# Mixture-of-experts kernel: VectorE makes both parts of two input groups, and two other groups are transposed ahead of the second routing step

## The chip, the core and the metric

The kernel runs on one core of a Trainium2 chip as one program. The metric is the device time of one execution in microseconds (us), lower is better. Engines are named as the profile names them: PE is TensorE (matmuls and transposes, its weight loads are PEld), DVE is VectorE, ACT is ScalarE, POOL is GpSimd and SP is SyncE, which here only issues DMAs.

## What is computed

The reference is a chain of two layers, each a conditioning stage and a feed-forward stage. The part that matters here is the second layer's conditioning, a mixture of experts with a shared branch:

```python
shared_out = silu(x_flat @ sw1.T) * (x_flat @ sw3.T) @ sw2.T
s = sigmoid(x_flat @ router_w.T + t_bias)            # 4096 tokens, 8 experts
topk_idx = top_k(s + router_bias, 2)
gates = s[topk_idx] / sum(s[topk_idx])
H = gelu(x_flat @ rw1[e].T); O = H @ rw2[e].T        # for the two experts of a token
out = (shared_out + sum_of_chosen(gates * O)) / 3
```

`x` is 16 sequences of 256 tokens of width 256. Before it come a recurrence of 256 steps with a router and a top-2 mixture of wide experts; after it a quantised feed-forward layer.

## The kernel before

The 4096 tokens are 32 tiles of 128 tokens, or 8 groups of 4 tiles. The recurrence takes up about the first 400 us, the first mixture's expert tiles run to 760 us, the second mixture from 760 to about 1000, and the quantised layer to the end. Each engine runs its own instruction stream in the order in which the program writes it; semaphores are the only ties between the engines. In the second mixture that order is written out by hand, in `mixture_pe`, `mixture_act`, `mixture_dve` and `mixture_pool`.

What happens to a group g before the expert tiles:

- SP loads `x1`, the layer's input, in 16 halves of groups (two per group, 256 KB each, L2071), at most four in flight.
- The input is split in two f16 parts. `input_hi` (L996, ACT) writes the high part of each half group and counts `xn_hi`; `input_lo` (L1208, DVE) waits for it, writes the low part and counts `xn_lo`. When eight low parts are done SP also loads the held expert weights, 2 MB, over the part of `x1` that was read (L2084).
- `transposes` (L846, PE) turns both parts, through two PSUM banks, and `input_T` (L1007, ACT) copies each back, counted by `xs_T`. A bank is free for the next group once its copy is made.
- `router` (L833, PE) multiplies the transposed group by the router's weights.

Routing goes in three steps over groups 0 to 1, 2 to 3 and 4 to 7. A step is 30 DVE operations (`mix_route_op`, L1128 to L1191): operation 0 reads the router's sums; ACT's `sigmoid` (L1053) comes between operations 0 and 1; after operation 14 PE's `mix_ranks` (L864, L868) counts the tokens of each expert, which operation 26 (L1178) reads; operation 29 (L1191) writes `mslot_of`, the destinations of the step's tokens. Then POOL scatters the rows of its groups to the experts' places in memory, 8 indirect DMAs a group, 64 in all (L1634), in the order of the groups.

The shared branch is cut in units: units 0 to 7 are the four pairs of hidden parts of group 0 (even units times `sw1`, odd ones times `sw3`). PE computes a unit into one of four banks. For an even unit ACT applies Silu (L1024, with a table load ahead of the first), for an odd unit DVE multiplies (L1229, waits for the Silu and for PE), then ACT makes the high part of the result (`hi_part`, L1014, issued behind the next even unit's Silu) and DVE the low part (`lo_part`, L1214). Units 8 and 9 belong to group 1, units 10 to 13 are outputs of group 0.

From unit 40 on PE takes up the expert tiles, 39 slots of tokens of one expert, with the remaining units between them. SP loads a tile's rows (L2115, or L2110 and L2112) once the scatters of groups 0 to 5 have landed (48 of the 64); PE transposes (L936) or takes a DMA transpose, computes both products (L833), DVE weighs the output with the gates (L1319) into one of three buffers, and POOL scatters it by up to two indirect DMAs (L1642, 71 in all). A buffer is free when its scatter has landed. When all 71 have landed SP loads the results back (L2132), DVE combines them, and the quantised layer follows.

## Time and profile before

| | |
|---|---|
| time, median of 3 runs | 1107.3 us (1105.65 to 1110.83) |
| time of the profiled execution | 1105.51 us, its span 1103.7 |
| busy PE, weight loads | 951.4 us (86%), 749.5 (68%) |
| busy DVE, ACT, POOL | 774.1 (70%), 542.8 (49%), 374.3 (34%) |
| mean granted clock of TensorE | 0.821 of full speed |
| input loads of the second mixture | from 765 us |
| its first expert tile | 856 us |
| results loaded back | from 972 us |

The busy shares are averages over stages with different limits. The chain of work that ended last is followed back from the last instruction, at each step to what released it. A row of a timeline gives start, length, engine, line, operation, tensors and count, and in brackets the idle time just before and what ended it. The granted clock is a share of 2.4 GHz, 0.50 is 1.2 GHz.

### The profile page before, as it was taken

Reading aid. Unit: us, or ns where it says so; the run is one execution under the profiler, and the core shown is the slowest. Engines: PE = TensorE matmul, PEld = TensorE weight load, DVE = VectorE, ACT = ScalarE, POOL = GpSimd, SP = SyncE. Lnnn points to the kernel's source line nnn. Section 1 sums busy time; section 2 is a strip of 40 time slices with the busy share of each in tenths; the row PEclk is TensorE's granted clock in tenths of the full one; section 3 lists DMA queues with packets and bytes.
Section 4 is the critical chain, followed back from the end, with each engine's and each line's share of the span. In section 5 each row is a group of like instructions: output and inputs, shape, how many; then the busy total and the mean of one; then the engine's idle time right before and its main releaser. Section 6 shows DMA issues by size and latency. Waiting matters only on the chain.

```text
span 1103.7 us, 29587 instructions
## 1 busy us (share of the span) xinstructions
PE 951.4 (86%) x9662; PEld 749.5 (68%) x9663; DVE 774.1 (70%) x2791; ACT 542.8 (49%) x1764; POOL 374.3 (34%) x412
## 2 busy tenths in 40 slices
PE   6777777777777699999999999997789999896787
PEld 5566665666656588888888888886455666573354
DVE  5676767767677676889656566654673697778977
ACT  4555555555555533333334334434643666536496
POOL 1001121211212356743433233332477667721000
PEclk7555555555555699999999999998899999998999
DMA  8322332323323345954843453544635779583024
GB/s 247 93 83 77 100 94 79 116 78 101 94 78 116 107 86 105 209 103 92 148 69 57 63 67 58 67 69 96 211 108 182 181 180 204 153 287 114 1 39 115
DMA packets 136266, 124.91 MB, mean 113 GB/s; under 512 B 80161, under 2 KB 115746, under 8 KB 135938
## 3 DMA queue, kind: packets, MB, share of 16 engines
q1 hardware_dynamic: 115010, 83.36, 29.6%
q0 software_dynamic: 21120, 39.77, 16.0%
q8 instruction: 80, 1.31, 0.5%
q14 instruction: 56, 0.46, 0.1%
HBM read 62.88 MB, written 56.87 MB: 109 GB/s over the span
## 4 chain that ended last, share of the span: by engine, by line
PE 55%; DVE 18%; ACT 10%; issue 7%; POOL 5%; DMA 4%; SPq 0%; DVEq 0%; POOLq 0%
PE ps L1706 15%; PE ps L1716 15%; PE ps L2349 8%; DVE ps L2276 6%; PE ps L2354 5%; PE ps L833 4%; ACT work L2200 4%; ACT ps L2195 4%; POOL mrows L1634 3%; DVE imax L1542 3%; PE ps L1438 2%; PE ps L2319 2%; POOL mresults L1642 2%; PE ps L2327 1%; DVE lane L1814 1%
## 5 line engine op out<-in xcount | busy, mean ns | idle before, releaser
L1735 ACT ACTIVATE lane<-ps,b_now 128x256 f32<-128x256 f32 (+1 forms) x312 | 141.0, 455 | 239.2 <-PE ps L1706 223.1
L1706 PE MATMUL ps<-lane,W 128*128 128x256 f16 (+1 forms) x1872 | 197.6, 264 | 1.5 <-issue 0.9
L1716 PE MATMUL ps<-W,lane 128*128 x1704 | 192.9, 273 | 0.8 <-DVE lane L1814 0.5
L1706 PEld LDWEIGHTS ps<-lane,W 128*128 x1872 | 170.9, 98 | 24.2 <-issue 4.1
L1716 PEld LDWEIGHTS ps<-W,lane 128*128 128x128 f16 x1704 | 165.3, 98 | 22.2 <-issue 1.7
L1896 POOL DMA_INDIRECT results<-lane,dest x71 | 113.8, 1603 | 194.5 <-DVE lane L1800 136.6
L2349 PE MATMUL ps<-work 128*128 128x16 f16 x2048 | 98.9, 177 | 86.7 <-ACT work L2200 86.1
L2349 PEld LDWEIGHTS ps<-work 128*128 128x128 f16 x2048 | 76.2, 107 | 138.3 <-ACT work L2200 136.9
L1814 DVE TENSOR_TENSOR lane<-lane 128x256 f16<-128x256 f32 (+1 forms) x312 | 125.7, 403 | 10.8
L1866 POOL DMA_INDIRECT rows<-work,slot_of x64 | 63.5, 992 | 156.4 <-DVE ps L2276 152.4
L1812 DVE CAST lane<-lane 128x256 f16<-128x256 f32 (+1 forms) x312 | 92.5, 297 | 20.3 <-ACT lane L1735 20.0
L2292 DVE TENSOR_TENSOR work<-ps,work 128x32 f16<-128x32 f32 x256 | 49.0, 191 | 78.3 <-ACT ps L2202 78.1
L2319 PE MATMUL ps<-work 128*128 128x128 f32 x256 | 97.7, 487 | 5.8 <-DVE work L2240 4.9
L2276 DVE TENSOR_TENSOR_SCAN ps<-ps,work 128x64 f32<-128x64 f32 x256 | 76.4, 299 | 30.6 <-ACT ps L2195 7.9
L833 PE MATMUL ps<-W,work 128*128 128x512 f16 x384 | 91.4, 385 | 3.3 <-issue 2.5
L2259 DVE SCALAR_TENSOR_TENSOR work<-ps,alpha,work 128x16 f32<-128x16 f32 x510 | 93.4, 225 | 0.0
L2195 ACT ACTIVATE ps<-ps 128x32 f32<-128x32 f32 x256 | 46.6, 182 | 93.9 <-PE ps L2354 93.9
L2200 ACT ACTIVATE work<-ps 128x32 f16<-128x32 f32 x256 | 50.6, 198 | 75.2 <-DVE ps L2276 73.9
L1800 DVE SCALAR_TENSOR_TENSOR lane<-ps,b_now 128x512 f32<-128x512 f32 (+1 forms) x39 | 25.1, 643 | 88.5 <-PE ps L1716 88.5
L1642 POOL DMA_INDIRECT mresults<-lane,mdest x71 | 72.5, 1021 | 28.1 <-issue 15.6
L2190 ACT ACTIVATE W<-stage 128x128 f16<-128x128 f32 x256 | 78.7, 307 | 0.0
L2300 DVE SCALAR_TENSOR_TENSOR W<-stage,W 128x128 f16<-128x128 f32 x256 | 71.7, 280 | 0.0
(299 smaller groups left out, 1548.8 us busy)
## 6 DMA issues: line engine op xcount, KB each, us to landing
stage<-in_w1T SPq DMA_DIRECT2D x16, 512.0 KB, 3.8
stage<-in_w2T SPq DMA_DIRECT2D x16, 512.0 KB, 4.2
b_now<-in_b SPq DMA_DIRECT2D x39, 128.0 KB, 2.9
W<-mrows SPq DMA_DIRECT2D x16, 260.0 KB
work<-in_zT SPq DMA_DIRECT2D x32, 128.0 KB, 2.2
results<-in_xn SPq DMA_DIRECT2D x32, 128.0 KB
W<-results SPq DMA_DIRECT2D x16, 256.0 KB, 4.1
W<-mresults SPq DMA_DIRECT2D x4, 1024.0 KB, 9.2
```

What stands on the lines that cost most here:

```text
L833: last = pe.matmul(dst, lhs(a, k), rhs(b, k), start=(n == 0 and k == ks[0]), stop=(n == 2 and k == ks[-1]))
L1642: pool.indirect_dma_start(out=mresults_d, in_=mout[:, b, q], in_offset=None, out_offset=bass.IndirectOffsetOnAxis(ap=mdest[:, n % GATE_BUF ...
L1706: last = pe.matmul(ps[:, f % 4, 0:wide], of_e(W1[:, bass.ds(e, 1), a, k, f * P:(f + 1) * P]), xrows[:, b, k], start=(i == 0 and k == 0), s ...
L1716: last = pe.matmul(ps[:, 4 + q, 0:D], hid[:, a, f, q * P:(q + 1) * P], of_e(W2[:, bass.ds(e, 1), b, f]), start=(i == 0 and f == 0), stop=( ...
L1735: act.activation(v4[:, f % 4, 0:wide], ps[:, f % 4, 0:wide], ACT.Relu, bias=b1_now[:, p, f:f + 1], scale=A_SCALE / W_SCALE).then_inc(l1_v, 1)
L1814: dve.tensor_tensor(lo, v, hi, ALU.subtract).then_inc(l1_hid, 1)
L1896: pool.indirect_dma_start(out=results_d, in_=obuf[:, p, q], in_offset=None, compute_op=ALU.add, out_offset=bass.IndirectOffsetOnAxis(ap=de ...
L2200: act.activation(hring[:, j % 2, 0, :, c:c + BATCH], u[:, :, :, 1], ACT.Tanh, scale=0.5)\
L2259: dve.scalar_tensor_tensor(zs[:, j % 2, c // BATCH, k, :, 1], h[:, k], alpha[:, k:k + 1], z[:, j, k, c:c + BATCH], ALU.mult, ALU.add).then ...
L2276: dve.tensor_tensor_scan(ps[:, 5, 0:2 * DB], ps[:, 6, 0:2 * DB], zs[:, j % 2, s % STEPS_PER_TILE].rearrange("p c b v -> p (c b v)"), 0.0, ...
L2319: pe.matmul(dst, wz[:, k, cols], z[:, slot, k, :], start=(k == 0), stop=False, skip_group_check=True)
L2349: pe.matmul(ps[:, b + m, c:c + BATCH], w[:, k, m * P:(m + 1) * P], hring[:, prev, 0, k, pc:pc + BATCH], start=False, stop=False, skip_grou ...
```

## The change

Six edits, all in the order of the second mixture before its expert tiles.

1. The high parts of groups 2 and 3 (halves 4 to 7) are made by DVE in `input_lo`, by a tensor_scalar ahead of each low part, and counted by a semaphore of their own, `xn_hi_v`. ACT no longer makes them. `hi_set` gives the semaphore and the count for a half.
2. DVE takes the inputs of groups 0 to 3 ahead of step 0 of the routing; before, groups 2 and 3 came behind it.
3. DVE stops after operation 14 of step 0 for units 0 and 1; before, they came behind the whole step and the low parts of groups 2 and 3.
4. DVE takes the low parts of groups 4 and 5 ahead of step 1; before, those of 4 to 7 came behind it. Those of 6 and 7 come behind it now.
5. PE transposes groups 2 and 3 ahead of unit 0, and groups 4 and 5 ahead of `mix_ranks(1)`; the units and `mix_ranks(0)` stand around them as the diff shows.
6. ACT copies the transposes of groups 2 and 3 and makes the high parts of groups 4 and 5 ahead of unit 0; it copies groups 4 and 5 ahead of `sigmoid(1)`, and makes the high parts of 6 and 7 behind it, ahead of unit 4.

```diff
+        def hi_set(i):
+
+            if i < 4:
+                return xn_hi, i + 1
+            return (xn_hi_v, i - 3) if i < 8 else (xn_hi, i - 3)
...
-                        pe.wait_ge(xn_lo if s else xn_hi, 2 * g + h + 1)
+                        pe.wait_ge(*((xn_lo, 2 * g + h + 1) if s else hi_set(2 * g + h)))
...
             for g in (0, 1):
                 router(g)
-            units(0, 3)
-            mix_ranks(0)
-            units(3, 4)
             for g in (2, 3):
                 transposes(g)
-            units(4, 5)
+            units(0, 2)
+            mix_ranks(0)
             for g in (2, 3):
                 router(g)
-            units(5, 7)
-            mix_ranks(1)
-            units(7, 8)
+            units(2, 4)
             for g in (4, 5):
                 transposes(g)
-            units(8, 9)
+            units(4, 7)
+            mix_ranks(1)
+            units(7, 9)
             for g in (6, 7):
                 transposes(g)
             units(9, 10)
...
             sigmoid(0)
             for g in (2, 3):
-                input_hi(g)
-            units(0, 2)
-            for g in (2, 3):
                 input_T(g)
-            units(2, 4)
-            sigmoid(1)
             for g in (4, 5):
                 input_hi(g)
-            units(4, 6)
+            units(0, 4)
+            for g in (4, 5):
+                input_T(g)
+            sigmoid(1)
             for g in (6, 7):
                 input_hi(g)
-            for g in (4, 5):
-                input_T(g)
-            units(6, 8)
+            units(4, 8)
             for g in (6, 7):
                 input_T(g)
...
-                    dve.wait_ge(xn_hi, i + 1)
+                    if 4 <= i < 8:
+                        dve.wait_ge(x_in[i % 4], 16 * (i // 4) + 16)
+                        dve.tensor_scalar(rows_[:, :, 0:D], x1[:, 2 * i:2 * i + 2], A_SCALE, None, ALU.mult).then_inc(xn_hi_v, 1)
+                    dve.wait_ge(*hi_set(i))
...
-            for g in (0, 1):
+            for g in (0, 1, 2, 3):
                 input_lo(g)
-            ops(0, 0, MIX_OPS)
-            for g in (2, 3):
+            ops(0, 0, 15)
+            units(0, 2)
+            ops(0, 15, MIX_OPS)
+            for g in (4, 5):
                 input_lo(g)
-            units(0, 2)
             ops_and_units(1, 2, 3, 4, 5)
-            for g in (4, 5, 6, 7):
+            for g in (6, 7):
                 input_lo(g)
```

## Rows read from the trace of the kernel before

**Rows 1.** Chain of work that ended last, 740 us to the end, by line.

```profile
by line: PE ps L833 13.3%; issue 11.4%; POOL mrows L1634 10.6%; DVE imax L1542 7.8%; PE ps L1438 5.6%; POOL mresults L1642 5.2%; DMA mresults<-lane,mdest 3.0%; DMA stage<-mresults 2.8%; PE ps L1426 2.5%; PE ps L1716 2.2%; DMA results<-lane,
```

**Rows 2.** POOL's timeline, 757 to 1000 us (start, length, operation, idle before).

```profile
784.57 1.19 POOL L1634 DMA_INDIRECT mrows<-W,mslot_of  x1 [21.73 <-DVE mslot_of L1191]
...
801.27 1.50 POOL L1634 DMA_INDIRECT mrows<-W,mslot_of  x1 [0.30 <-issue]
...
848.18 1.01 POOL L1634 DMA_INDIRECT mrows<-work,mslot_of  x1 [0.30 <-issue]
...
884.88 0.97 POOL L1642 DMA_INDIRECT mresults<-lane,mdest  x1 [3.07 <-DVE lane L1319]
```

**Rows 3.** POOL by line, 784 to 870, 870 to 896, 896 to 971 us: busy, idle before.

```profile
L1634 POOL DMA_INDIRECT mrows<-W,mslot_of x32 | 34.0, 1062 | 31.2 <-DVE mslot_of L1191 21.7 <-issue 8.8 <-DVE W L1154 0.6
L1634 POOL DMA_INDIRECT mrows<-work,mslot_of x32 | 32.1, 1004 | 9.8 <-issue 9.8
...
L1642 POOL DMA_INDIRECT mresults<-lane,mdest x16 | 16.0, 999 | 10.2 <-DVE lane L1319 6.9 <-issue 3.4
...
L1642 POOL DMA_INDIRECT mresults<-lane,mdest x56 | 57.5, 1026 | 18.2 <-issue 12.5 <-DVE lane L1319 3.8 <-DVE mdest L1300 1.8
```

**Rows 4.** SP's timeline, and L2071's issue to landing.

```profile
774.21 4.96 SPq L2071 DMA_DIRECT2D W<-results  x6
...
786.84 0.36 SPq L2084 DMA_DIRECT2D W<-rweights  x1
...
852.00 0.39 SPq L2115 DMA_DIRECT2D W<-mrows  x1
...
DMA to landing us min/median/max: 2.8/4.1/4.5
```

**Rows 5.** PE's timeline, 757 to 880 us.

```profile
800.26 1.97 PE L846 MATMUL ps<-identh,work 128*128 128x128 f16 x16 [3.07 <-DVE work L1208]
...
809.24 2.56 PE L833 MATMUL ps<-rw_s,W 128*128 128x8 f16 x96
...
856.31 0.61 PE L936 MATMUL ps<-identh,W 128*128 128x128 f16 x8
```

**Rows 6.** ACT's timeline, 757 to 880 us.

```profile
773.45 1.94 ACT L1007 ACTIVATE W<-ps 128x1024 f16<-128x1024 f16 x2 [0.21 <-PE ps L846]
...
776.71 2.17 ACT L996 ACTIVATE W<-W 128x512 f16<-128x512 f32 x4
778.90 1.28 ACT L1024 ACT_TABLE_LOAD   x1
780.19 0.60 ACT L1024 ACTIVATE lane<-ps 128x512 f32<-128x512 f32 x1
...
790.46 0.26 ACT L1053 ACTIVATE W<-W 128x64 f32<-128x64 f32 x1 [0.62 <-DVE W L1128]
```

**Rows 7.** DVE's timeline, 757 to 880 us.

```profile
770.78 1.36 DVE L1208 SCALAR_TENSOR_TENSOR W<-W 128x512 f16<-128x512 f32 x2 [0.84 <-ACT W L996]
776.29 0.23 DVE L1128 SCALAR_TENSOR_TENSOR W<-ps,t_bias 128x64 f32<-128x64 f32 x1 [4.15 <-PE ps L833]
...
780.48 0.29 DVE L1154 TENSOR_TENSOR W<-W 128x128 f32<-128x128 f32 x1
...
784.12 0.17 DVE L1191 CAST mslot_of<-W 128x16 uint32<-128x16 f32 x1
...
799.43 4.90 DVE L1208 SCALAR_TENSOR_TENSOR work<-W,work 128x512 f16<-128x512 f32 x8
...
811.84 0.29 DVE L1128 SCALAR_TENSOR_TENSOR W<-ps,t_bias 128x128 f32<-128x128 f32 x1 [0.24 <-PE ps L833]
```

**Rows 8.** DVE by line and shape, whole span: count, busy, mean ns.

```profile
L2241 DVE TENSOR_SCALAR work<-work 128x512 f16<-128x512 f32 x1 | 0.4, 419 | 0.0
```

**Rows 9.** Stretches: length, busy PE, PEld, DVE, ACT, POOL; clock, DMA share, GB/s.

```profile
776.00:779.00 3.00, 3.00 (x17) 1.12 (x15) 2.04 (x10) 2.44 (x6) 0.00 (x0) 0.50 0.92 260
...
776.00:812.00 36.00, 27.42 (x332) 17.20 (x330) 26.18 (x84) 24.27 (x36) 21.64 (x20) 0.90 0.51 171
```

More of the change, by code:

```diff
@@ L462, in build_program @@
         xn_hi = sem("xn_hi")
+        xn_hi_v = sem("xn_hi_v")
         xn_lo = sem("xn_lo")
```

## The prediction

> **What bounds the kernel now.** I read the chain of work that ended last from 740 us on, then each engine's timeline over 757 to 880 us, then GpSimd's (POOL's) own queue to the end of the mixture. The chain view shows that POOL's scatter instructions of L1634 are, with 10.6%, the second largest named part of the last 364 us and that those of L1642 add 5.2% [rows 1]. POOL's timeline says why: it issues nothing until the destinations of step 0 are there (21.73 us idle, first scatter at 784.57), and from then on one every 1.28 us [rows 2]. The grouped rows count 64 of L1634 and 71 of L1642 and little idle time other than the 0.30 us between issues; only between 870 and 896 does POOL wait for VectorE (DVE), 6.9 us, and 3.8 us after that [rows 3]. So two serial things run side by side: POOL's 135 scatters, which start when step 0 of the router is done, and TensorE (PE), which reaches the tiles at 856.31 without idle time [rows 5]. They meet twice. SyncE (SP) may load the rows of tile 0 only when 48 scatters have landed; the 48th is issued at 848.18 and SP's load at 852.00 [rows 2, 4]. And at the end 71 results must be out. PE is the pacemaker of the tiles until about 896, where POOL waits for it; before the tiles it has slack only as far as tile 0's rows allow, at most 856.31 - 852.00 = 4.3 us for their landing.
>
> **The change part by part.** All times are those of the profiled run (span 1103.7, time 1105.51, 1.8 below the median of 1107.3); the difference found is added to the median.
>
> *VectorE's new operations.* Four tensor_scalar of 128x512 f32 to f16. The same form takes 419 ns at L2241 [rows 8]; about 0.04 us of waiting for its own semaphore follows, and the low part goes on at 4.90 / 8 = 0.61 us each [rows 7]. So 4 x (0.46 + 0.61) = 4.3 us, begun when the low parts of groups 0 and 1 are done, about 772.1 (770.78 + 1.36) [rows 7]. The data is there: SP's load 10 (counted from 0), issued at 774.21, waited for load 6, so the last of the four halves lands about 774.9 and none is later than DVE's turn by more than 0.1 us [rows 4]. DVE ends at 776.4; today it waits 4.15 us for the router until 776.29 [rows 7]. Cost 0.1 us, cover complete. If the operation ran at the pace of the low part (0.69 us) it would cost 1.2 us; below nothing is excluded, since step 0 can't begin before the router's sums.
>
> *ScalarE (ACT) is relieved of* the four high parts of groups 2 and 3 (2.17 us at 776.71) [rows 6], but what follows matters more. Today it goes on to the table load (1.28) and the first Silu, done at 780.79 [rows 6]. Now it does sigmoid(0) until 776.8 (today its next operation starts at 776.71), then four copies of transposes, then the four high parts of groups 4 and 5, and only then units 0 and 1. PE makes the first half of group 2's transposes from 776.1 at the low clock (granted 0.50, so 1.2 GHz) [rows 9], 8 in 1.05 us; copies follow at 777.2, 778.3, 779.4 and 780.4, PE and ACT taking turns as they do for group 1 (two copies in 1.94 us) [rows 6], and end at 781.4. High parts until 783.5, table load until 784.8, Silu until 785.4.
>
> *Destinations of step 0.* DVE now stops after 15 operations of step 0 for units 0 and 1. Unit 1 needs that Silu: 785.4 instead of no wait at all, for DVE reached this place at 780.48. It takes 0.61 us, and the other 15 operations take 784.29 - 780.48 = 3.8 us [rows 7]. Destinations at 789.8, first scatter at 790.1 instead of 784.57: **+5.5 us** on POOL. PE is not what ends this wait: its units 0 and 1 are done at 783 at the high clock, at 785.5 if the clock stayed low, so the term holds either way within 0.5 us.
>
> The rows give the table load 1.28 us with the Silu right behind it [rows 6]. The Trainium skill (ScalarE: Activation LUTs, What ACT_TABLE_LOAD costs) adds a drain of about 1.38 us to each switch. This trace doesn't show that part; by the page the term would be 6.9 us.
>
> *Step 1 and 2 behind it.* Low parts of groups 4 and 5 (2.45 us) end at 792.3; PE waits for the first of them inside transposes(4), from 787.9 to 790.5. ACT's last copy of group 5 ends at 794.4, sigmoid(1) starts there instead of 790.46 [rows 6]. From sigmoid(1) to the end of step 1 is 9.0 us today (790.46 to 799.43) [rows 6, 7]; unchanged, since the extra unit waits are met: destinations at 803.4. POOL needs them 16 scatters after 790.1, at 811. Then low parts of 6 and 7 (2.45), unit 5 and its high part (1.2), four copies (4.1), router of groups 4 to 7 (2.56) [rows 5] and hand-overs: the first operation of step 2 at about 814.0 instead of 811.84 [rows 7], destinations some 11 us later (30 operations, an estimate from their spacing of 0.26 to 0.35 us in this timeline), at 825; POOL needs them 32 scatters after 790.1, at 833 [rows 3]. Both are covered, by 8 us each.
>
> *TensorE.* Of 36 us from 776 to 812 it is busy 27.42 [rows 9], 8.6 idle. In the new order I find idle 2.6 (transposes(4)), 1.1 (group 5), 1.8 (mix_ranks(1) at 798.9), 1.9 (transposes(6)) and 3.4 us (transposes(7), whose copy stands behind unit 6's high part on ACT), 10.8 in all: **+2.2 us** at the tiles, 858.5. After 3.07 us idle today, 16 transposes took 1.97 us [rows 5]; one or two such slow stretches may add 1 us each. They are covered by the next term.
>
> *Tile 0's rows.* The 48th scatter moves by 5.5 less what POOL's pace gains. Two scatters of 1.50 us lie beside the eight low parts of 799.43 (the one of 801.27 stands for both) [rows 2, 7]; today 12 low parts run beside POOL's scatters, then 8. I take 0.5 us off, bounds 0 and 1.1 (both long ones gone). The Trainium skill (SBUF — State Buffer, Who interferes with whom) says that such an operation with two SBUF inputs contends only with a GpSimd instruction that reads SBUF, and a tensor_scalar in its two-port mode with any; by it the new operations harm nothing, as POOL is idle then, and the gain would be nothing or all of it. SP's load of tile 0 goes to 857.0. Its landing isn't in the trace: at most 4.3 us as above; the 256 KB loads of x took 2.8 to 4.5 [rows 4]. I take 3.5, as scatters run beside it: rows at 860.5, PE at 856.3 + **4.2** (2.9 to 5.5).
>
> *SP.* The 2 MB load at 786.84 [rows 4] waits for eight low parts, now done at 776.4, and goes out behind the last x load, about 782.7. It ends before most scatters: nothing on the path.
>
> *End.* From the tiles to 896 PE paces and POOL waits for it, so the last scatter moves with PE, and the loads, the combination and the last stage follow serially. Sum +4.2: 1107.3 + 4.2 = **1111.5**.
>
> **Rivals.** (a) *POOL's own pace decides* (slower): the tiles' rows and every mout buffer hang on POOL, so the whole +5.5 arrives, or 6.9 with a longer way to the Silu: 1112.8 to 1114.5. For it: 56 scatters after 896 go almost without a wait [rows 3]. Against it: 10.7 us of waits for DVE since 870. It decides if the shift of the first scatter is over 5.5.
> (b) *The delay is absorbed* (not slower): if POOL waits less between 870 and 896 as it comes later (up to 6.9 us there) and tile 0's rows take 2.8 us, only PE's own shift is left; if PE's gaps also come out smaller than mine, that shift is 0 to 2.2: 1107.3 to 1109.5. For it: the slack is in the rows. Against it: tile 0 hangs on scatter 48, ahead of the slack.
> (c) *Faster*: sooner transposes fill PE's gaps and the Silu isn't late, so destinations come at 784.3 as now. Of the 8.6 us idle the 3.07 before transposes(4) [rows 5] would go: 1104.2. It needs ACT to reach unit 0 by 779.2, and its queue forbids that.
> (d) *Nothing of the order matters*, within 1 us of 1107.3: would need step 0's second half to be off every chain; the 21.73 us wait for it speaks against it.
>
> **Chances.** Forecast (+2.5 to +5.5) 0.55; (a) 0.23; (b) with (d) 0.16; (c) 0.06. About 0.5%, 5.5 us, is what a measurement of this kernel can tell from no change. Over that slower: all of (a) above 1112.8, and a little of the forecast's edge, 0.27; faster by it: only a (c) larger than found, 0.04; within: 0.69. The range leaves out (c) and the upper end of (a) by noise: 1107.0 to 1114.5.
>
> **What would show it.** First scatter near 790.1 and a DVE wait of about 4.8 us for ScalarE ahead of unit 1; high parts by DVE of about 0.42 us between 772 and 776.4; SP's load of tile 0 near 857; an idle time of about 2 us of PE ahead of the first tile transposes; the last scatter near 974. The prediction is wrong if unit 1 is read before 782, if the load of tile 0 goes out before 854, or if PE reaches the tiles later than its rows.

## The result, and the profile after

| | before | after |
|---|---|---|
| time, median of 20 runs each | 1106.95 us (1104.99 to 1110.83) | 1109.88 us (1107.22 to 1111.28) |
| ratio after to before | | 1.0020, 95% interval 1.0011 to 1.0028 |
| time of the profiled execution, its span | 1105.51, 1103.7 | 1109.46, 1107.5 |

By the ratio the change costs 2.2 us (1.2 to 3.1). The two medians are 2.9 us apart; here and below a cost in us is worked out from the ratio, which has the interval. The forecast was +4.2, 1111.5, on a base of 1107.3: the direction was right, the size was about twice what came and lies outside the interval. The prediction took some 5.5 us as the least that a measurement of this kernel can tell from no change; with 20 runs each the interval is about 1 us to either side. Of all executions below one, of pe_late, fell in a slow state (1181.64 us); it stands in that run's median and in no ratio.

One thing for every comparison below: the stages before the second mixture don't end at the same time in two executions. I take the start of DVE's copy that opens the second mixture as a mark and subtract its offset. In the profile after the offset is 0.64 us. "Net" means with the offset taken off; the rows are raw.

POOL's timeline of after: start, length, operation, idle before. The first scatter comes at 790.17 net instead of 784.57 [rows 2], 5.6 us later.

```profile
790.81 1.19 POOL L1639 DMA_INDIRECT mrows<-W,mslot_of  x1 [27.12 <-DVE mslot_of L1192]
792.30 1.50 POOL L1639 DMA_INDIRECT mrows<-W,mslot_of  x1 [0.30 <-issue]
...
852.53 0.96 POOL L1639 DMA_INDIRECT mrows<-work,mslot_of  x1 [0.30 <-issue]
...
972.11 0.97 POOL L1647 DMA_INDIRECT mresults<-lane,mdest  x1 [0.31 <-issue]
```

DVE's timeline of after. The four high parts take 0.42 us each (one row stands for them), operation 0 starts behind them without a wait, and unit 1 waits 4.85 us for the Silu. The change has moved DVE's wait from ahead of step 0 (4.15 us, [rows 7]) to the middle of it.

```profile
773.94 0.42 DVE L1210 TENSOR_SCALAR W<-W 128x512 f16<-128x512 f32 x1
...
777.13 0.21 DVE L1129 SCALAR_TENSOR_TENSOR W<-ps,t_bias 128x64 f32<-128x64 f32 x1
...
786.14 0.69 DVE L1233 SCALAR_TENSOR_TENSOR W<-ps,lane 128x512 f32<-128x512 f32 x1 [4.85 <-ACT lane L1029]
...
790.36 0.17 DVE L1192 CAST mslot_of<-W 128x16 uint32<-128x16 f32 x1
...
804.33 0.17 DVE L1192 CAST mslot_of<-W 128x16 uint32<-128x16 f32 x1
...
816.22 0.29 DVE L1129 SCALAR_TENSOR_TENSOR W<-ps,t_bias 128x128 f32<-128x128 f32 x1 [1.75 <-PE ps L840]
...
826.24 0.18 DVE L1192 CAST mslot_of<-W 128x32 uint32<-128x32 f32 x1
```

ACT's timeline of after. Four copies, the high parts of groups 4 and 5, the table load and only then the Silu that DVE waits for, as its queue has them.

```profile
777.98 1.94 ACT L1012 ACTIVATE W<-ps 128x1024 f16<-128x1024 f16 x2 [0.35 <-PE ps L853]
780.13 1.94 ACT L1012 ACTIVATE W<-ps 128x1024 f16<-128x1024 f16 x2 [0.21 <-PE ps L853]
781.96 2.18 ACT L1001 ACTIVATE work<-W 128x512 f16<-128x512 f32 x4
784.16 1.28 ACT L1029 ACT_TABLE_LOAD   x1
785.45 0.60 ACT L1029 ACTIVATE lane<-ps 128x512 f32<-128x512 f32 x1
```

PE's timeline of after: the idle times ahead of the transposes, and the first tile.

```profile
791.28 1.97 PE L853 MATMUL ps<-identh,work 128*128 128x128 f16 x16 [3.23 <-DVE work L1212]
...
799.93 0.21 PE L871 MATMUL ps<-m_m,tri 128*128 128x72 bf16 x1 [1.49 <-DVE m_m L1153]
...
805.24 0.91 PE L853 MATMUL ps<-identh,work 128*128 128x128 f16 x8 [1.86 <-DVE work L1212]
809.13 1.95 PE L853 MATMUL ps<-identh,work 128*128 128x128 f16 x16 [2.98 <-ACT W L1012]
810.87 2.77 PE L840 MATMUL ps<-W,work 128*128 128x512 f16 x6
...
860.70 0.61 PE L941 MATMUL ps<-identh,W 128*128 128x128 f16 x8
```

Stretches of after (length, busy PE, PEld, DVE, ACT, POOL; granted clock, DMA share, GB/s), the first from 776 net to just ahead of step 2's routing, the last from 776 net to the tiles. Behind the idle times of 1.86 and 2.98 us PE is busy throughout 810 to 818, at 1.2 GHz (0.50): six matmuls of 512 columns take 2.77 us there.

```profile
776.64:816.04 39.40, 29.19 (x336) 19.27 (x332) 24.13 (x80) 22.44 (x32) 19.74 (x19) 0.80 0.45 153
810.00:818.00 8.00, 8.00 (x122) 5.74 (x121) 2.56 (x6) 3.25 (x5) 6.14 (x7) 0.50 0.31 108
776.64:860.70 84.06, 72.11 (x604) 45.74 (x601) 45.93 (x142) 37.70 (x63) 53.73 (x54) 0.87 0.47 155
```

SP's timeline of after: the load of tile 0, and the results loaded back.

```profile
856.13 0.39 SPq L2120 DMA_DIRECT2D W<-mrows  x1
...
974.59 0.94 SPq L2137 DMA_DIRECT2D W<-mresults  x2
```

### The profile page after: what moved, and what is told of

Same layout as the page of the kernel before. It is cut to its first block, busy times and chain, and to the rows that moved or that the text cites. A ratio compares the mean times of both kernels' runs of the same rounds, so it can differ in the third digit from the quotient of the medians.

```text
span 1107.5 us, 29578 instructions
## 1 busy us (share of the span) xinstructions
PE 957.9 (86%) x9653; PEld 755.3 (68%) x9663; DVE 775.1 (70%) x2795; ACT 540.5 (49%) x1760; POOL 369.3 (33%) x412
## 4 chain that ended last, share of the span: by engine, by line
PE 57%; DVE 19%; ACT 11%; issue 6%; DMA 4%; POOL 3%; SPq 0%; DVEq 0%; POOLq 0%
PE ps L1711 15%; PE ps L1721 15%; PE ps L2354 8%; PE ps L840 7%; DVE ps L2281 6%; PE ps L2359 5%; ACT work L2205 4%; ACT ps L2200 4%; DVE imax L1547 3%; POOL mresults L1647 3%; PE ps L1443 2%; PE ps L2324 2%; DVE lane L1819 1%; PE ps L2332 1%; PE ps L1431 1%
## 5 line engine op out<-in xcount | busy, mean ns | idle before, releaser
L1901 POOL DMA_INDIRECT results<-lane,dest x71 | 114.1, 1606 | 193.7 <-DVE lane L1805 140.9
L1819 DVE TENSOR_TENSOR lane<-lane 128x256 f16<-128x256 f32 (+1 forms) x312 | 125.6, 402 | 10.8
L1647 POOL DMA_INDIRECT mresults<-lane,mdest x71 | 70.2, 989 | 28.5 <-issue 17.4
L2305 DVE SCALAR_TENSOR_TENSOR W<-stage,W 128x128 f16<-128x128 f32 x256 | 71.4, 279 | 0.0
```

Of the source, the lines that this page charges most:

```text
L1647: pool.indirect_dma_start(out=mresults_d, in_=mout[:, b, q], in_offset=None, out_offset=bass.IndirectOffsetOnAxis(ap=mdest[:, n % GATE_BUF ...
L1819: dve.tensor_tensor(lo, v, hi, ALU.subtract).then_inc(l1_hid, 1)
L1901: pool.indirect_dma_start(out=results_d, in_=obuf[:, p, q], in_offset=None, compute_op=ALU.add, out_offset=bass.IndirectOffsetOnAxis(ap=de ...
```

## The experiments

All times are against runs of the kernel before, made beside them on the same chip. There are 12 runs each of pool_late, pe_late, whole_step0 and silu_first, 8 to 11 of whole_and_silu, three_moves and dve_part, four each of clock_kept and low_twice, and one of before, again. Two theories run through the expectations: P, that the end follows POOL's chain of 135 scatters, and E, that it follows PE's arrival at the tiles. The table gives, net of the start offset, what each profile shows at the places of the forecast's sum; "long" is the number of the 135 scatters that took over 1.2 us, and the sum of what all of them took over 0.97.

| kernel | ratio, interval | first scatter | PE at tiles | scatter 81 | scatter 135 | 81 to 135 | long |
|---|---|---|---|---|---|---|---|
| before | | 784.57 | 856.31 | 896.41 | 969.43 | 73.0 | 13, 7.6 |
| before, again | | 785.11 | 858.25 | 898.34 | 970.41 | 72.1 | 11, 6.5 |
| after | 1.0020 (1.0011 to 1.0028) | 790.17 | 860.06 | 900.59 | 971.47 | 70.9 | 6, 3.7 |
| pool_late | 1.0035 (1.0021 to 1.0050) | 790.91 | 859.56 | 900.98 | 972.07 | 71.1 | 6, 3.9 |
| pe_late | 1.0030 (1.0015 to 1.0045) | 785.29 | 861.69 | 902.01 | 973.58 | 71.6 | 9, 5.1 |
| whole_step0 | 0.9971 (0.9957 to 0.9984) | 784.86 | 855.84 | 896.47 | 967.92 | 71.5 | 6, 4.1 |
| silu_first | 0.9993 (0.9980 to 1.0006) | 788.20 | 856.87 | 897.57 | 969.43 | 71.9 | 7, 3.9 |
| whole_and_silu | 0.9975 (0.9959 to 0.9992) | 784.92 | 856.60 | 896.96 | 968.31 | 71.4 | 5, 2.9 |
| three_moves | 0.9970 (0.9959 to 0.9980) | 785.95 | 854.30 | 896.51 | 967.84 | 71.3 | 4, 3.1 |
| dve_part | 0.9994 (0.9985 to 1.0003) | 784.77 | 854.86 | 895.33 | 966.88 | 71.6 | 8, 4.7 |
| clock_kept | 1.0040 (1.0025 to 1.0056) | 790.34 | 860.01 | 901.70 | 974.07 | 72.4 | 10, 5.5 |
| low_twice | 1.0100 (1.0078 to 1.0123) | 790.16 | 865.35 | 907.37 | 981.84 | 74.5 | 9, 6.2 |

### POOL alone comes late, PE alone comes late

Before, with POOL's first group waiting for operation 0 of step 1 too, which delays the scatters and nothing else directly:

```diff
-                pool.wait_ge(router_step, MIX_OPS * (step_of(g) + 1))
+                pool.wait_ge(router_step, MIX_OPS * (step_of(g) + 1) + (g == 0))
```

> The kernel before, with one thing added: POOL's first scatter also waits for operation 0 of step 1, so it starts about 790.6 instead of 784.6 (+6 us); every other engine keeps its order. Theory P (what arrives at the end is the delay of POOL's chain of 135 scatters): tile 0's rows come at about 861, PE waits for them some 4 us, the last scatter and the end move by 4 to 6 us, ratio 1.004 to 1.005. Theory E (PE's arrival at the tiles decides, and POOL's delay is covered by slack): 0 to +1 us, ratio 1.000 to 1.001.

Measured: 1111.82 against 1107.52 us, ratio 1.0035, +3.9 us. POOL's timeline:

```profile
792.63 1.19 POOL L1634 DMA_INDIRECT mrows<-W,mslot_of  x1 [27.87 <-DVE W L1128]
```

PE's timeline:

```profile
861.28 0.61 PE L936 MATMUL ps<-identh,W 128*128 128x128 f16 x8 [1.42 <-DMA W<-mrows]
```

SP's timeline:

```profile
858.04 0.39 SPq L2115 DMA_DIRECT2D W<-mrows  x1
```

Before, with three of the units computed twice on PE ahead of the tiles, the second result over the first:

```diff
                     c, weights = w // 2, (sw1s, sw3s)[w % 2]
+                    for _ in range(v in (29, 30, 31)):
+                        split_matmul(ps[:, unit_bank(v)], lambda s, k: weights[:, s, k, c * P:(c + 1) * P],
+                                     lambda s, k: xs[:, g, s, k], range(DC))
                     last = split_matmul(
```

> The kernel before, with three units of the shared branch computed twice on PE (18 more matmuls of 512 columns, 3.9 us) ahead of the tiles; POOL's start and pace untouched. PE reaches the tiles 3.9 us later, at about 860.2, and the rows of tile 0 are there by then. Theory E: the end moves by the whole 3.9 us, or by about 2 if POOL gives back what it gave back in the changed kernel between the tiles' first and last scatter: ratio 1.002 to 1.0035. Theory P: nothing, since POOL's scatters end as before: 1.000.

Measured: 1112.17 us, ratio 1.0030, +3.3 us. POOL's timeline:

```profile
786.30 1.19 POOL L1637 DMA_INDIRECT mrows<-W,mslot_of  x1 [22.27 <-DVE mslot_of L1194]
```

PE's timeline:

```profile
862.70 0.61 PE L939 MATMUL ps<-identh,W 128*128 128x128 f16 x8
```

Each cause alone gives a loss at least of the size of the whole change. With POOL late by 6.3 us PE stands 1.42 us in front of the tiles and waits for the rows. SP issued their load at 858.04 (856.32 net), so they landed 3.2 us later. That is neither theory's number: P had PE wait some 4 us and a ratio of 1.004 to 1.005, E had no more than 1.001. With PE late by 5.4 us (3.9 expected) and POOL on time nothing waits for rows, and the last scatter is late by 4.1; the ratio is inside E's 1.002 to 1.0035 and not P's 1.000. So the end doesn't hang on POOL's start alone. In pool_late the delay shows at the tiles as a wait for tile 0's rows, and there 4.3 us less 3.2, some 1.1 us, were free: SP's load of tile 0 moved by 4.3 us and PE by 3.2.

### Undoing the stop inside step 0

After, with step 0 whole:

```diff
-            ops(0, 0, 15)
-            units(0, 2)
-            ops(0, 15, MIX_OPS)
+            ops(0, 0, MIX_OPS)
+            units(0, 2)
```

> The changed kernel, with DVE doing all 30 operations of step 0 before units 0 and 1 (edit 3 undone, the others kept). First scatter back at about 785 to 785.5 instead of 790.8; PE's order and its late arrival at the tiles (about 860) stay. Theory P: the whole loss goes, ratio to the kernel before 1.000. Theory E: the loss stays, 1.002, since POOL's start had slack.

Measured: 1105.27 against 1107.52 us, ratio 0.9971, 3.2 us faster than before. POOL's timeline:

```profile
786.29 0.99 POOL L1638 DMA_INDIRECT mrows<-W,mslot_of  x1 [21.84 <-DVE mslot_of L1192]
```

DVE's timeline:

```profile
785.84 0.17 DVE L1192 CAST mslot_of<-W 128x16 uint32<-128x16 f32 x1
787.02 0.69 DVE L1233 SCALAR_TENSOR_TENSOR W<-ps,lane 128x512 f32<-128x512 f32 x1 [1.01 <-PE ps L840]
```

PE's timeline:

```profile
857.27 0.61 PE L941 MATMUL ps<-identh,W 128*128 128x128 f16 x8
```

The wait of 4.85 us for the Silu is gone; by the time DVE reaches unit 1 only 1.01 us of waiting is left, for PE. The first scatter is at 784.86 net. Three lines of the change thus cost more than the whole loss (1.0020 to 0.9971), and what is left of the change is a gain. Neither theory gave that: P had 1.000 and E 1.002, as both had PE stay near 860. But PE came to the tiles at 855.84 net, 4.2 us sooner than in after. DVE's stop held the low parts of groups 4 and 5 too, for which PE waits before it transposes (3.23 us in after), so this run takes two delays out at once, POOL's and PE's, and doesn't tell which of them was the loss.

### The Silu sooner in ACT's queue

After, with ACT's units 0 and 1 ahead of the high parts of groups 4 and 5:

```diff
+            units(0, 2)
             for g in (4, 5):
                 input_hi(g)
-            units(0, 4)
+            units(2, 4)
```

> The changed kernel, with ACT taking units 0 and 1 ahead of the high parts of groups 4 and 5 instead of behind them. The Silu is done 2.2 us sooner, the first scatter goes out at about 788.6 instead of 790.8, step 1's chain is 2 us shorter too (transposes(4) wait for the low part 2 us less), so PE arrives at the tiles about 1.5 to 2 us sooner. Both theories: part of the loss goes, ratio to the kernel before 1.000 to 1.001; it tells whether the order of ACT is where the loss is made.

Measured: 1106.40 against 1107.52 us, ratio 0.9993, no difference from before. DVE's timeline:

```profile
783.49 0.69 DVE L1234 SCALAR_TENSOR_TENSOR W<-ps,lane 128x512 f32<-128x512 f32 x1 [2.77 <-ACT lane L1029]
```

POOL's timeline:

```profile
788.17 1.18 POOL L1640 DMA_INDIRECT mrows<-W,mslot_of  x1 [25.30 <-DVE mslot_of L1193]
```

DVE's wait falls from 4.85 to 2.77 us, by about the high parts that now stand behind, and the first scatter is 2.0 us sooner than in after. So it is the order of ACT's queue that makes the wait, as the row's releaser, `lane L1029`, says. PE reaches the tiles at 856.87 net, 3.2 us sooner than in after, where 1.5 to 2 were expected. The first scatter is still 3.6 us later than in before, PE only 0.6 us, and the time is that of before.

### The two edits together, and a third

After, with both edits above:

> The kernel after with two edits: DVE makes step 0 whole before units 0 and 1, and ACT makes units 0 and 1 ahead of the high parts of groups 4 and 5. It stands between whole_step0 (the first edit alone, 0.9971 of before) and three_moves (both and a third, 0.9970). Theory A, the end follows the time at which PE reaches the tiles: with step 0 whole the first scatter is near 785 already, so the early Silu can't bring it sooner; it only fills PE's gaps before 812, and PE at the tiles comes near 855, time 1104 to 1105.5. Rival B, POOL's start decides: the first scatter is the same as in whole_step0, so the time is that of whole_step0 within 0.3 us, 1105.3, whatever PE does. In both the profile should have fewer than 10 scatters over 1.2 us.

Measured: 1106.35 against 1108.83 us, ratio 0.9975 (0.9959 to 0.9992). PE reached the tiles at 856.60, not near 855, and the time lies above both expectations (1104 to 1105.5 and 1105.3), on a base that is 1.3 us higher than whole_step0's. The early Silu added nothing to the whole step 0, so the two theories aren't told apart by this run. What it does show is that the Silu mattered only through the stop in step 0. Beside silu_first, which is this kernel with the stop, it shows more: the stop makes the first scatter 3.3 us later (788.20 against 784.92) and PE at the tiles no more than 0.3 (856.87 against 856.60), and the ratio is 0.9993 against 0.9975. That would be 2 us for POOL's late start alone, but the intervals overlap.

The same with one move more: DVE takes unit 5 ahead of the inputs of groups 6 and 7:

```diff
+            units(5, 6)
             for g in (6, 7):
                 input_lo(g)
-            units(5, 10)
+            units(6, 10)
```

> The changed kernel with three moves: DVE does step 0 whole before units 0 and 1, ACT takes units 0 and 1 ahead of the high parts of groups 4 and 5, and DVE takes unit 5 ahead of the low parts of groups 6 and 7, so that ACT's high part of unit 6's pair no longer waits behind them and transposes(7) need not wait 2.98 us. First scatter at 785, PE at the tiles 2 to 3 us sooner than with the first move alone (855.8), at about 853.5, where tile 0's rows (SP's load at about 850) may just be there. Theory E (PE's arrival decides): 2 us below the first move's kernel, ratio to the kernel before 0.995. Theory P (POOL's chain decides): no better than the first move's kernel, 0.997.

Measured: 1104.22 against 1107.31 us, ratio 0.9970. PE's timeline:

```profile
854.75 0.61 PE L941 MATMUL ps<-identh,W 128*128 128x128 f16 x8 [0.17 <-DMA W<-mrows]
```

PE is at the tiles 2.0 us sooner than in before and even waits 0.17 us for rows, and yet the last scatter is within 0.1 us of whole_step0's (967.84 and 967.92) and the times agree within the intervals. That is theory P's 0.997, not E's 0.995, the other way round than in pe_late. Three versions (whole_step0, whole_and_silu, three_moves) are 0.25 to 0.30% faster than before; the runs don't rank them.

### VectorE's part alone

Before, with edits 1 and 2 of the change only: DVE makes the high parts of groups 2 and 3 and takes both groups ahead of step 0; all other orders as before.

```diff
-            for g in (2, 3):
-                input_hi(g)
             units(0, 2)
...
-            for g in (0, 1):
+            for g in (0, 1, 2, 3):
                 input_lo(g)
             ops(0, 0, MIX_OPS)
-            for g in (2, 3):
-                input_lo(g)
             units(0, 2)
```

> The kernel before with edits 1 and 2 of the change alone: DVE makes both parts of groups 2 and 3 while it waits for the router, ACT no longer makes their high parts; PE's order, units and step 0 stay. First scatter at about 784.8 (+0.2); DVE is free 2.4 us sooner after step 0, so the low part of group 2 and ACT's Silu no longer hold transposes(2) and (3) (1.14 and 0.67 us of PE idle before), and step 1 starts up to 2 us sooner. PE at the tiles 1 to 2 us sooner. Theory E: ratio 0.998 to 0.999. Theory P: 1.000.

Measured: 1106.77 against 1107.31 us, ratio 0.9994. PE's timeline:

```profile
855.90 0.61 PE L943 MATMUL ps<-identh,W 128*128 128x128 f16 x8
```

The destinations of step 0 don't move (+0.2 us), which is the forecast's 0.1 for this part. PE is 1.4 us sooner at the tiles and the last scatter 2.5 sooner in the profile, but of that the median shows no more than 0.5 us. The interval (0.9985 to 1.0003) takes in P's 1.000 and the upper part of E's 0.998 to 0.999.

### The clock kept up

After, with 12 matmuls of 256 columns, whose results nothing reads, behind each half of group 6's transposes, into a free bank, so that PE doesn't stand idle ahead of group 7:

```diff
                     last.then_inc(in_T, 1)
+                    if g == 6:
+                        pe.wait_ge(router_step, MIX_OPS + 1)
+                        for _ in range(12):
+                            pe.matmul(ps[:, 2, 256:512], tri[:], ones16[:, 0:1].broadcast_to([P, 256]), start=True, stop=True)
```

> The changed kernel with 24 matmuls of 256 columns that serve nothing, in the two places where PE waits 1.86 and 2.98 us around the transposes of group 6; 2.6 to 3 us of work in 4.8 us of waiting. If the granted clock of 0.50 from 810 to 818 came of that idle time, it stays at 1.00 here, PE works off the 818 to 832 stretch 3 to 4 us sooner and reaches the tiles at about 857 instead of 860; the end moves by 1 to 3 us, ratio to the kernel before 1.000. If the clock falls anyway, the matmuls only add: 1.003.

Measured: 1111.89 us, ratio 1.0040, +4.4 us, slower than after itself. Stretches, the first from 776 net to the tiles:

```profile
778.89:862.90 84.01, 71.81 (x633) 45.62 (x631) 47.41 (x144) 37.70 (x63) 53.81 (x53) 0.93 0.46 154
810.00:818.00 8.00, 6.15 (x131) 5.14 (x132) 3.29 (x7) 5.56 (x8) 6.17 (x7) 1.00 0.31 110
```

PE's timeline:

```profile
811.55 0.62 PE L853 MATMUL ps<-identh,work 128*128 128x128 f16 x8 [1.65 <-ACT W L1016]
...
836.96 5.40 PE L840 MATMUL ps<-work,W 128*128 128x256 f16 x48 [1.40 <-DVE W L1222]
...
862.90 0.61 PE L945 MATMUL ps<-identh,W 128*128 128x128 f16 x8 [1.47 <-DMA W<-mrows]
```

The fill did what it was for: the clock is 1.00 in 810 to 818 instead of 0.50, and eight transposes behind it take 0.62 us, where after takes 1.95 for 16. But from 776 net to the tiles PE needs 84.01 us, as in after (84.06). What the clock gave went into waits for DVE (0.77, 1.40 and 0.73 us, of which after has 1.01 and 0.73 too) and for the rows (1.47). So the low clock of after isn't a loss that can be had back alone; DVE and tile 0's rows stand right behind it. The expectation, PE at the tiles near 857 and a ratio of 1.000, missed. That the run is slower than after arises behind the tiles: from scatter 81 to the last it takes 72.4 us instead of 70.9, 0.8 of them because more scatters are long; for the rest no run shows the cause.

### Twice the low parts

After, with 28 of the 32 low parts computed twice into the same place:

```diff
                 hid_ = hid_of(h // HSC)
+                if 4 <= h:
+                    link(dve, dve.scalar_tensor_tensor(hid_[:, 1, h % HSC], vs[:, h % 3], V_SCALE / (2 * MIX_SCALE),
+                                                       hid_[:, 0, h % HSC], ALU.mult, ALU.subtract))
                 dve.scalar_tensor_tensor(hid_[:, 1, h % HSC], vs[:, h % 3], V_SCALE / (2 * MIX_SCALE), hid_[:, 0, h % HSC],
```

> The kernel after, in which DVE computes each low part from the fifth on (28 of 32) twice, into the same place, 0.61 us each, 17 us of DVE in all, spread over 796 to 960; DVE is 70% busy. It asks whether a scatter that is issued beside such an operation of two SBUF inputs is held by it. Theory C, it is: the trace of after has 6 of 135 scatters over 1.2 us, each beside a low part; with twice the time of low parts the number is near 12 (9 to 16), the sum of what scatters take over 0.97 us goes from 3.7 to about 6.5 us, and part of it arrives at the end: 1110 to 1114. Rival, the long scatters are a matter of chance or of the scattered addresses: their number stays 6 within 2, and the others don't lie beside low parts. If DVE's own extra time paces the tiles, the time rises by more, up to 17 us, and shows as waits of PE or POOL for DVE; the count of long scatters tells the theories apart all the same.

Measured: 1120.07 against 1108.83 us, ratio 1.0100. POOL by line and shape (count, busy, mean ns, idle before):

```profile
L1650 POOL DMA_INDIRECT mresults<-lane,mdest x71 | 71.9, 1013 | 36.4 <-DVE lane L1327 18.5 <-issue 16.5 <-DVE mdest L1308 1.5
```

PE's timeline:

```profile
839.45 6.84 PE L840 MATMUL ps<-work,W 128*128 128x256 f16 x48 [3.45 <-DVE W L1221]
```

The scatters take 6.2 us over 0.97 each instead of 3.7, near the 6.5 expected, and all nine over 1.2 us lie beside a low part. Their number is at the lower end of what was expected, and it doesn't tell the theories apart: clock_kept, with each low part once, has ten and 5.5 us. What tells them apart is where the long ones lie and how long they are, in all profiles; it stands in the last section. The time rose by 11 us, more than my range, and PE now waits for DVE ahead of the tiles (3.45 us here, 1.82 at a second place). The run says nothing on what the long scatters cost at the end.

### Before once more

One more profile of the unchanged kernel, to see how much of a difference between two traces is the execution:

> The kernel before, unchanged, for a second profile of it. Theory C (a scatter of POOL is held up to 0.53 us when a low part of DVE, which reads two tensors from SBUF, runs as it is issued; how many are hit depends on how the two timelines meet): the same program meets in the same way, so again 12 or 13 scatters over 1.2 us, every one beside a low part, and some 73.0 us from scatter 81 to 135. Theory N (the long scatters of the first profile were chance): some 6, and about 71.2 us as in the other kernels.

Measured: 1110.32 us, a single run in the upper part of what before takes, span 1108.5, 4.8 us above the first profile's. Eleven long scatters and 72.1 us lie nearer to theory C (12 or 13, 73.0) than to N (6, 71.2), and nine of the eleven are the same scatters as in the first profile. The stretch from 776 net to the tiles, which PE reached at 858.25 net:

```profile
777.82:860.07 82.25, 69.87 (x611) 43.33 (x612) 47.82 (x144) 39.52 (x67) 56.37 (x56) 0.91 0.52 162
```

The stretch from 776 net to the tiles in before:

```profile
776.00:856.31 80.31, 67.41 (x597) 41.87 (x595) 47.86 (x144) 39.43 (x67) 55.58 (x54) 0.96 0.49 163
```

The first profile needs 80.31 us for that stretch with 67.41 busy, at a granted clock of 0.96; this one needs 82.25 with 69.87 busy, at 0.91. The same program reached the tiles 1.9 us later, busier by 2.5 us at a lower clock. In the profile on which the forecast rests PE came to the tiles early.

## Why the prediction was wrong, and what of it held

**In short.** Two steps failed. The first is "the last scatter moves with PE", +4.2: it moved by 2.0. The second is the way to +4.2 at the tiles: the sum had PE wait there for tile 0's rows, and PE came later than its rows, which the prediction itself named as a sign that it is wrong. That the figure at the tiles is near (+3.75) is in part luck.

**The first half held.** Net of the offset, against the forecast:

| step | forecast | measured |
|---|---|---|
| high part on DVE | 0.42 | 0.42 |
| operation 0 of step 0, moved by | 0.1 | 0.2 |
| table load ends, Silu ends | 784.8, 785.4 | 784.8, 785.4 |
| DVE waits for the Silu | 4.8 | 4.85 |
| first scatter | 790.1 (+5.5) | 790.17 (+5.6) |
| destinations of steps 1 and 2 | 803.4, 825 | 803.7, 825.6 |
| PE idle until step 2's router sums | 10.8 (+2.2) | 10.2 (+1.6) |
| first operation of step 2 | 814.0 | 815.58 |
| SP's load of tile 0 | 857.0 (+5.0) | 855.49 (+3.5) |
| landing of tile 0's rows | 3.5 us | 3.2 us (in pool_late) |
| PE at the tiles | 860.5 (+4.2), by rows | 860.06 (+3.75), by itself |
| scatter 81 | +4.2 | +4.2 |
| last scatter | +4.2 | +2.0 |

The stop inside step 0 is the cause of the loss: taking it out alone turned the loss into a gain (whole_step0), and shortening the wait by moving the Silu took back the loss (silu_first). The rows give the table load 1.28 us with the Silu 0.01 us behind it (784.16, 785.45), as in before. The drain of about 1.38 us that the Trainium skill (ScalarE: Activation LUTs, What ACT_TABLE_LOAD costs) adds to a switch appears in neither trace; with it the Silu would have ended at 786.8.

**Tile 0's rows: the figure near, the reason wrong.** I had PE wait for rows at 860.5, as POOL's pace would give back 0.5 us (bounds 0 and 1.1). It gave back 1.9, beyond my bound: over the first 64 scatters the excess over 0.97 us was 4.0 us in before (3.0 in its second profile) and is 2.3 in after. So the rows had landed by about 858.7 (855.49 and the 3.2 us of pool_late), and PE didn't wait for them at 860.06. PE itself was later than my 858.5. Over the whole stretch to the tiles its idle time didn't grow but fell by about 1 us (11.95 against 12.90), while it was busy 4.7 us longer (72.11 against 67.41) at a mean clock of 0.87 against 0.96. A part of that belongs to this order: the 0.50 of 810 to 818 comes again in low_twice, which is the same kernel up to there, and in none of the other ten profiles, where that stretch is at 0.73 or more. A part may be the single execution, as before, again was busy for 2.5 us more than the first profile. I had written that the slow stretches may add 1 us each and are "covered by the next term"; they weren't covered, they took that term's place. That PE can't simply have this time back is what clock_kept shows.

**The end: this is the term that was mis-sized.** I wrote that "the last scatter moves with PE", +4.2. Until scatter 81 the shift is +4.2. From there to the last it is POOL that sets the pace, one scatter behind another with little idle time, and this POOL ran faster than in before: 70.9 us against 73.0. POOL by line and shape in after, for the 56 scatters that [rows 3] show at a mean of 1026 ns and 57.5 us of busy time:

```profile
L1647 POOL DMA_INDIRECT mresults<-lane,mdest x56 | 55.2, 986 | 18.2 <-issue 14.3 <-DVE lane L1324 3.3 <-DVE mdest L1305 0.6
```

That is 2.3 us less busy time for the same 56 instructions. With it the last scatter is late by 2.0 us, not 4.2. My third row of [rows 3] showed the slow mean; I read its idle time and not its length. The last column but one of the table bears this out: from scatter 81 to 135 before takes 73.0 us, 3.0 of them excess over 0.97, and after 70.9, 0.9 of them excess; what is left is 70.0 in both. It lies between 69.4 and 70.6 in all profiles but low_twice (72.1). Nor is the gain chance alone: the two profiles of before have 13 and 11 long scatters, mostly the same ones (numbers 2, 5, 13, 14, 76, 87, 116, 127 and 132 in both), and are the two highest sums of all the kernels; any shift of POOL against DVE, even pool_late's, which touches nothing else, lowers the sum to between 2.9 and 5.5, low_twice apart. Before had the unlucky meeting of the two timelines, and a change that moves them gets out of it; that this one did was luck and not design. All this is strong evidence, though no run took the long scatters away by themselves.

**The base.** The forecast's difference was taken against one trace, and that trace was early at the tiles. Against the second profile of before, the last scatter of after is 1.1 us late, against the first 2.0; the +2.2 us of the 20 runs is of that order. What between the return of the results and the end differs (132.9 us in after, 131.7 and 133.3 in the two profiles of before) is the scatter of single executions.

**The rivals.** (a), POOL's own pace decides, +5.5 or more, is refuted by the first scatter at +5.6 with a time of +2.2, and by pe_late, which has next to no POOL delay (0.7 us) and costs 3.3; its upper figure should also be 1114.2, from the 6.9, and not 1114.5. (b), the delay is absorbed, gave 0 to +2.2 and is, at its upper edge, where the time came out, but not by its way: the slack of 870 to 896 absorbed nothing (scatter 81 at +4.2). What absorbed was POOL's pace, ahead of the tiles and behind 896. One part of (b) did hold: only PE's own shift was left at the tiles, but it was 3.75 us and not up to 2.2. (c) needed the Silu in time, and ACT's queue forbade it, as said. Its other half, that the rest of the order is worth something, is true: whole_step0 runs it without the stop. (d), nothing of the order matters, falls with after against whole_step0, whose intervals (1.0011 to 1.0028 and 0.9957 to 0.9984) are apart.

**What stays open.** The links aren't additive. From PE's arrival at the tiles to the last scatter it is 111.4 to 114.1 us in eleven of the twelve profiles (116.5 in low_twice), and why three_moves and dve_part, both at the tiles 1.4 to 2.0 us sooner than before, gain so unequally (3.1 and 0.5 us by the medians) isn't settled. Nor is it settled how the loss of after divides between POOL's late start and PE's late arrival: POOL's alone costs 3.9 us for 6.3 in pool_late and perhaps 2 for 3.3 in silu_first beside whole_and_silu, PE's alone 3.3 us for 5.4 in pe_late, and in after both are there.

## What to carry to other kernels

When an engine's wait is filled by cutting a serial chain, look at what the inserted work waits for on the *other* engine's queue: here three lines put a Silu, with four copies, four high parts and a table load before it, into the middle of the chain that feeds 64 serial scatters, and ahead of low parts that PE waits for, and without them the change is a gain of 0.3%. Carry a shift to the end only as far as the next place where another engine sets the pace, and ask there how long its instructions take, not only how idle it is. Take the base from two profiles of the unchanged kernel when the difference is under 0.5%: two of them here were 1.9 us apart at the tiles.

## What the hardware showed that I had not expected

**A scatter is held by an operation that reads two SBUF tensors, and by how much is set by when it comes.** An indirect scatter takes 0.97 us. Issued up to about 0.5 us after the start of a low part it is held until the same moment, and ends about 1.53 us after the low part's start. In all twelve profiles together 134 scatters are issued so, and all of them end 1.52 to 1.55 us after that start. The timeline of all engines in before, around two low parts and, between them, the multiply of an odd unit (L1229), the same operation and as long, but with one of its two tensors in PSUM:

```profile
839.88 0.69 DVE L1214 SCALAR_TENSOR_TENSOR W<-W 128x512 f16<-128x512 f32 x1 [7.43 <-ACT W L1014]
839.95 1.47 POOL L1634 DMA_INDIRECT mrows<-work,mslot_of  x1 [0.31 <-issue]
...
856.98 0.68 DVE L1229 SCALAR_TENSOR_TENSOR W<-ps,lane 128x512 f32<-128x512 f32 x1
857.14 0.97 POOL L1634 DMA_INDIRECT mrows<-work,mslot_of  x1 [0.30 <-issue]
...
888.53 0.69 DVE L1214 SCALAR_TENSOR_TENSOR W<-W 128x512 f16<-128x512 f32 x1
888.82 1.24 POOL L1642 DMA_INDIRECT mresults<-lane,mdest  x1 [0.30 <-issue]
```

And in after:

```profile
893.00 0.68 DVE L1218 SCALAR_TENSOR_TENSOR W<-W 128x512 f16<-128x512 f32 x1
893.29 1.23 POOL L1647 DMA_INDIRECT mresults<-lane,mdest  x1 [0.30 <-issue]
...
908.72 0.68 DVE L1218 SCALAR_TENSOR_TENSOR W<-W 128x512 f16<-128x512 f32 x1
...
908.92 1.33 POOL L1647 DMA_INDIRECT mresults<-lane,mdest  x1 [0.31 <-issue]
```

Delays of 0.07, 0.20 and 0.29 us give lengths of 1.47, 1.33 and 1.24 (1.23 in after). Across before, after, pool_late and dve_part it goes on so: 0.42 gives 1.12, 0.53 gives 1.01, from 0.6 on it is 0.97, and a scatter issued before the low part begins takes 0.96 or 0.97 in nearly all cases. In the series of low parts of the input the operation that starts 0.02 to 0.05 us before a scatter holds it for the longest, 1.50 us (`792.30` above). Of the long scatters of all profiles one (pool_late) lies beside another operation, all others beside a low part.

Two more counts over the twelve profiles leave little room for chance or for the scattered addresses. Beside the multiply that reads PSUM and SBUF, 137 scatters are issued within 0.5 us of its start, and they take 0.97 us, 1.00 at most. The low part of an expert tile (L1310 in before) reads two SBUF tensors too, but takes 0.42 us: 65 scatters are issued 0.05 to 0.25 us after its start, and all end 0.84 us after its end, as those beside the low parts of 0.69 us do (0.84 to 0.87). So the operation's length sets the hold; the one that pool_late has over 1.2 us is of this kind.
**The clock differs between executions of one program.** Over 776 to 800 and 800 to 856 of the raw time the granted clock was 0.92 and 0.97 in one profile of before and 0.86 and 0.92 in the other, and PE was at the tiles 1.9 us later in the second, about as much as the change costs.
